# Graph network on one core: one-hots of sources kept in DRAM and read back in later rounds

## The chip, the cores and the metric

The program runs on one core of a Trainium2 chip. Its engines run beside each other and wait on semaphores: PE (matmuls, and transposes by an identity), DVE and ACT (elementwise work), POOL (here it issues the gathers) and SP (here it issues most loads and stores). Sixteen DMA engines move the data. The metric is the device time of one execution in microseconds (us); three runs took 7040.45, 7045.45 and 7043.78, median 7043.78.

## The reference

A graph of 3125 nodes with 64 features and 103,125 edges, sorted by destination, goes through four blocks, each followed by adding its input and a layer norm:

```python
norm = deg_inv[src] * deg_inv[dst]                       # 1 round: sum
out  = segment_sum(norm[:, None] * x[src], dst)
ke   = k[src] + edge_attr @ we                           # 2 rounds: attention
a    = exp(score - segment_max(score, dst)[dst])         # score = (q[dst] * ke).sum / 8
out  = segment_sum(a / denom[dst] * (v[src] + e), dst) + x @ ws + bs
msg  = (h @ weight)[src, rel_type] * edge_weight         # 1 round: relations
h    = relu(cat(x[dst], x[src] - x[dst]) @ W1 + b1) @ W2 + b2
x    = relu(segment_max(h, dst))                         # 3 rounds: maximum
```

Every round needs the row of each edge's source node, x[src], for all edges.

## The kernel before

Edges lie in 808 tiles of 128; four tiles make a chunk of 512 edges, 202 chunks in all. The attention rounds take one chunk a step (202 steps). The sum, relation and maximum rounds pair a chunk of the first half with one of the second and take 101 steps of eight tiles. Between rounds a stage works on the nodes in seven groups of blocks and writes the next round's table of source rows (src_table) and, for attention and maximum, of destination rows (dst_table).

A tile's source rows come in one of two ways. POOL gathers them by an indirect DMA, 128 rows of 256 bytes (`gather`, L1194, and `gather_att`, L1201). Or they are picked on PE: DVE compares the tile's 128 source numbers with all 25 x 128 node numbers and writes a one-hot of 128 x 3200 bytes in fp8 (`make_onehot`, L1752); PE multiplies its 25 blocks with the table, which lies in SBUF split into three bf16 parts (`split_table`, L851 to L854), into one PSUM bank (`pick`, L1456: 25 matmuls of 192 columns a tile); DVE adds the three parts and puts the rows where a gather would have (`place_rows`, L1763). The sum round picks one tile in eight from step 4 on; a maximum round picks one and two tiles in turn from step 1 on. Attention and relations gather everything. There are two buffers for one-hots.

The order on every engine is written out by `chunks`: in step t a stage with lag k works on chunk t - k, and the stages of a step stand in the order of the list. Waits are on semaphores, and an engine or a DMA queue that waits holds up all that stands behind it.

In an attention round SP's step for chunk c (`fetch_att`) loads the one-hots of destinations every fourth chunk (L1103), then four windows of destination rows (L1109), and for even c the edge features of chunks c and c + 1 (L1112). The last of these waits until DVE has weighed chunk c - 7, whose slot is reused:

```python
wait(sp, (q.weighted, c - UA + 2))      # UA = 8 slots
```

PE makes a chunk's queries from the windows (`query`, L1494); DVE multiplies them with keys (`product`, L1813); once a group of four chunks is through the softmax, DVE weighs a chunk's rows (`weigh`, L1877) and PE turns them (L1549); a scan over the edges follows (L1774), PE turns its result back (`back`, L1565), ACT copies it out and stores it. DVE weighs chunk c - 5 in the step in which it forms the product of chunk c.

Of the kernel before, what the change touches and what calls it, by code (L numbers as in the profile page):

```python
# [26 lines left out]
P = 128  # L27
TC = 4
# [3 lines left out]
CH = C // 2  # L32
# [30 lines left out]
PICKS = {"sum": (4, (1,)), "max": (1, (1, 2))}  # L63


def gnn_kernel(nc, src, typ, wgt, dst_row, dst_prev, dst_tile, first, edge_t, x, W, out):
# [21 lines left out]
    src_rows = dram("src_rows", (CH, 2, P), f32)  # L88
    states = [dram("states_sum", (EP, D), f32), dram("states_att", (EP, KA), f32)]

    ctx = ExitStack()
    with ctx:
# [3 lines left out]
        def sem(name):  # L96
# [21 lines left out]
        wrel = sb("wrel", [P, R, D])  # L118
# [51 lines left out]
                  for r, t in {0: flat_agg, 4: tab_a, 5: wide_x, 6: tab_a}.items()}  # L170
# [67 lines left out]
        pick_ps = ps[:, 4, 0:2 * PARTS * D]  # L238
        last_ids = ps[0:1, 6:8, :].rearrange("p b f -> p (b f)")
# [32 lines left out]
        cols_made, cols_turned, rows_made = sem("cols_made"), sem("cols_turned"), sem("rows_made")  # L272
        src_rows_stored = sem("src_rows_stored")
        table_split = sem("table_split")
        ids_copied = sem("ids_copied")
# [56 lines left out]
        class Round:  # L332

            def __init__(self, r, kind):
                self.r, self.kind = r, kind
                self.steps = CH if kind in PAIRED else C
                C_ = self.steps

# [37 lines left out]
                if kind == ATT:  # L376
                    self.rows_ready = [shared(f"rows_ready_a{s_}", 16 * TC * len(range(s_, C, UA))) for s_ in range(UA)]
# [6 lines left out]
                else:  # L384
                    self.first_pick, pattern = PICKS.get(kind, (C_, (0,)))
                    self.picks = [pattern[(c - self.first_pick) % len(pattern)] if c >= self.first_pick else 0
                                  for c in range(C_)]
                    self.most = max(pattern)
                    self.rows_ready = [shared(f"rows_ready_{s_}", self.gathered((C_ - 1 - s_) // U * U + s_))
                                       for s_ in range(U)]  # L390
                if kind in PICKS:
                    picks, self.span = sum(p > 0 for p in self.picks), PB // self.most
                    self.src_loaded = [shared(f"src_loaded_{h}", 16 * len(range(self.first_pick + h * self.span, C_,
                                                                                2 * self.span))) for h in range(2)]
# [16 lines left out]
            def gathered(self, c):  # L411

                return 16 * sum(2 * TC - self.picks[t] for t in range(c % U, c + 1, U))

            def before(self, c):

                return sum(self.picks[0:max(c, 0)])
# [1536 lines left out]
```

## Time and profile before

| | |
|---|---|
| Median of three runs | 7043.78 us |
| Profiled execution | 7051.56 us, span 7049.7 |
| Busy share of the span | POOL 72%, DVE 63%, PE 62%, ACT 23% |
| Gathers (L1194 and L1201) | 5109 |
| One-hots made (L1752) | 547, 1887.8 us of DVE |
| Pick matmuls on three tables (L1456) | 547 x 25 |
| Mean granted clock of PE | 0.767 |

The rounds follow one another with short node stages between: POOL's gathers of the results (L1223) begin at 986 us for the sum round and at 2043 for the first attention round, those of the second end at 3165; the relation round follows, and the three maximum rounds get their first rows at 4336, 5243 and 6150. In the profile's lines an engine's busy time says little by itself, since rounds differ; each round is read apart. "issue" is time in which an engine waited for nothing that the profile shows. SPq is an instruction of SP that issues a DMA; its duration is that of the issue, not of the transfer. A granted clock of 1.00 is 2.4 GHz, 0.50 is 1.2 GHz.

### The profile page before, as it was taken

How to read it: one execution, taken by the hardware profiler on the slowest of the kernel's cores; microseconds unless marked ns; L12 is line 12 of the kernel's file. 1: busy time of each engine (PE TensorE's matmuls, PEld its weight loads, DVE VectorE, ACT ScalarE, POOL GpSimd, SP SyncE). 2: the span in 40 equal slices, each digit the busy share in tenths (PEclk: the TensorE clock that was granted, in tenths of full speed). 3: DMA queues.
4: the chain of work that ended last, by engine and by line, in shares of the span. 5: the costliest groups of instructions: out<-in, count | busy, mean ns of one | idle time of the engine just before them, and what ended most of it. 6: DMA issues, size and time to landing. Idle time of an engine off the chain costs nothing. (4 is left out here: it accounts for less than half of the span.)

```text
span 7049.7 us, 104267 instructions
## 1 busy us (share of the span) xinstructions
PE 4355.2 (62%) x31312; PEld 3479.8 (49%) x31312; DVE 4410.3 (63%) x5581; ACT 1607.1 (23%) x2960; POOL 5057.5 (72%) x5327
## 2 busy tenths in 40 slices
PE   2555546666666556564111125888878888788886
PEld 2554545555565555552111113666656666566664
DVE  7777756666655666662122125777767777677777
ACT  0111113333332333332000001222222222222222
POOL 5777767777757777764777776777767777677776
PEclk9777766666665676666555556999989999899998
DMA  8666656777766777763222224655545655555554
GB/s 168 176 175 176 176 126 134 145 148 149 145 120 134 146 149 145 147 128 104 59 57 59 59 57 91 136 134 134 134 109 136 136 132 135 116 131 133 136 134 108
DMA packets 2145262, 901.73 MB, mean 128 GB/s; under 512 B 1793543, under 2 KB 2004660, under 8 KB 2138308
## 3 DMA queue, kind: packets, MB, share of 16 engines
q1 hardware_dynamic: 1065012, 466.62, 28.7%
q10 hardware_dynamic: 909808, 252.48, 15.8%
q0 software_dynamic: 169888, 175.97, 13.9%
q8 instruction: 259, 4.24, 0.3%
q14 instruction: 295, 2.42, 0.1%
HBM read 625.25 MB, written 269.09 MB: 127 GB/s over the span
## 5 line engine op out<-in xcount | busy, mean ns | idle before, releaser
L1194 POOL DMA_INDIRECT edges_a<-src_table,idx x3493 | 3325.0, 952 | 1287.6 <-issue 1063.4
L1752 DVE TENSOR_TENSOR early<-src_b,ps 128x3200 fp8e4<-128x3200 f32 x547 | 1887.8, 3474 | 576.1 <-PE ps L1456 500.2
L1201 POOL DMA_INDIRECT edges_a<-src_table,idx x1616 | 1530.6, 947 | 536.3 <-issue 458.9
L1470 PE MATMUL ps<-ident,edges_a 128*128 128x128 f32 x808 | 206.8, 405 | 1232.3 <-DVE edges_a L1795 836.7
L1456 PE MATMUL ps<-tab_a,early 128*128 128x192 bf16 x7500 | 699.6, 256 | 253.2 <-DVE edges_a L1763 234.5
L1456 PEld LDWEIGHTS ps<-tab_a,early 128*128 128x128 fp8e4 x7500 | 648.8, 102 | 307.0 <-DVE edges_a L1763 280.0
L1470 PEld LDWEIGHTS ps<-ident,edges_a 128*128 128x128 f32 x808 | 133.0, 202 | 1297.0 <-DVE edges_a L1795 878.2
L1813 DVE TENSOR_TENSOR prod<-ps,edges_a 128x388 f32<-128x388 f32 x404 | 224.9, 557 | 734.8 <-DMA edges_a<-src_table,idx 350.9
L1494 PE MATMUL ps<-win_sb 128*128 128x97 f32 x3232 | 645.4, 364 | 28.3 <-DMA win_sb<-dst_table 28.1
L1565 PE MATMUL ps<-ident,st 128*128 128x128 f32 (+1 forms) x3636 | 649.3, 314 | 5.9 <-DVE st L1774 5.7
L1565 PEld LDWEIGHTS ps<-ident,st 128*128 128x128 f32 (+1 forms) x3636 | 549.6, 176 | 168.0 <-issue 157.1
L1278 ACT ACTIVATE hb<-ps 128x512 f32<-128x512 f32 x505 | 296.2, 587 | 1435.7 <-PE ps L1565 1435.4
L1272 ACT ACTIVATE dst_b<-sel 128x1024 f32<-128x1024 fp8e4 x303 | 320.6, 1058 | 1301.9 <-DMA sel<-onehots 1212.2
L1494 PEld LDWEIGHTS ps<-win_sb 128*128 128x128 f32 x3232 | 597.5, 276 | 38.2 <-DMA win_sb<-dst_table 32.0
L1483 PE MATMUL ps<-dst_b,win_sb 128*64 128x128 f32 x4848 | 535.5, 299 | 0.0
L1795 DVE TENSOR_TENSOR edges_a<-edges_a,wgt_sb 128x256 f32<-128x256 f32 x202 | 77.5, 425 | 712.6 <-DMA edges_a<-src_table,idx 712.6
L1774 DVE TENSOR_TENSOR_SCAN st<-dst_b,st,ps 97x512 f32<-97x512 f32 x402 | 508.2, 1264 | 5.1 <-PE ps L1565 5.1
L1774 DVE TENSOR_TENSOR_SCAN st<-edges_a,st,ps 128x512 f32<-128x512 fp8e4 x200 | 255.7, 1279 | 355.0 <-PE ps L1470 229.7
L1549 PE MATMUL ps<-ident,weighted 128*97 128x128 f32 x1616 | 368.0, 367 | 169.4 <-DVE weighted L1877 167.8
L1456 PE MATMUL ps<-wide_x,early 128*128 128x192 bf16 x3750 | 349.6, 256 | 126.6 <-DVE edges_a L1763 117.5
L1456 PEld LDWEIGHTS ps<-wide_x,early 128*128 128x128 fp8e4 x3750 | 324.3, 102 | 153.4 <-DVE edges_a L1763 140.5
L1480 PE MATMUL ps<-ident,edges_a 128*128 128x128 f32 x1212 | 383.1, 316 | 15.6 <-DMA edges_a<-src_table,idx 15.6
(229 smaller groups left out, 5317.7 us busy)
## 6 DMA issues: line engine op xcount, KB each, us to landing
states_sum<-hb ACTq DMA_DIRECT2D x505, 256.0 KB
edges_a<-src_table,idx POOLq DMA_INDIRECT x5109
win_sb<-dst_table SPq DMA_DIRECT2D x1616, 48.5 KB
states_att<-hb ACTq DMA_DIRECT2D x202, 388.0 KB
dst_b<-in_dst_row SPq DMA_DIRECT2D x50, 1024.0 KB, 12.0
src_b<-src_rows SPq DMA_DIRECT2D x174, 256.0 KB
sel<-onehots SPq DMA_DIRECT2D x305, 128.0 KB
win_sb<-dst_table ACTq DMA_DIRECT2D x1212, 32.0 KB
```

Of the source, the lines that this page charges most:

```text
L1194: pool.indirect_dma_start(rows[:, u, j * D:(j + 1) * D], None, srcs[q.r], bass.IndirectOffsetOnAxis(ap=idx[:, h, at:at + 1], axis=0))\
L1201: pool.indirect_dma_start(xe_a[:, s, j * KA:j * KA + D], None, srcs[q.r], bass.IndirectOffsetOnAxis(ap=idx_a[:, s, j:j + 1], axis=0))\
L1272: nc.scalar.activation(sel_f[:, v, :], sel[:, v, 0:2 * EC], ACT.Copy).then_inc(q.sel_wide.sem, 1)
L1456: last = nc.tensor.matmul(pick_ps[:, at:at + PARTS * D], onehot_b[:, i % 2, b, :], tables[q.r][:, b, :, :].rearrange("p k f -> p (k f)"), ...
L1470: last = nc.tensor.matmul(bank(TURNED, s)[:, j * P:(j + 1) * P], rows[:, v, j * P:(j + 1) * P], ident[:, :], is_transpose=True, start=True ...
L1480: nc.tensor.matmul(bank(TURNED, s)[:, at_j], rows[:, s, j * P:(j + 1) * P], ident[:, :], is_transpose=True, start=True, stop=False)
L1483: last = nc.tensor.matmul(bank(TURNED, s)[h * D:h * D + D, at_j], win_pair(s, j, h), sel_f[:, s, h * EC + j * P:h * EC + (j + 1) * P], sta ...
L1494: last = nc.tensor.matmul(bank(TURNED, s)[:, j * KA:(j + 1) * KA], wide_a[:, s % V, j * P:(j + 1) * P], win_att(v, j), start=True, stop=True)
L1549: last = nc.tensor.matmul(bank(QUERY, s)[0:KA, j * P:(j + 1) * P], weighted[:, s % V, j * KA:(j + 1) * KA], ident[:, :], is_transpose=True ...
L1565: last = nc.tensor.matmul(bank(BACK, s)[:, j * w:(j + 1) * w], st[0:w, s % V, j * P:(j + 1) * P], ident[0:w, 0:w], is_transpose=True, star ...
L1752: nc.vector.tensor_tensor(onehot_b[:, i % 2, :, :], src_b[:, h, o:o + P].unsqueeze(1).to_broadcast([P, NB, P]), ids_ps.unsqueeze(2).to_bro ...
L1774: nc.vector.tensor_tensor_scan(st[0:w, s % V, :], d0, d1, init, op0, op1).then_inc(q.st_ready.sem, 1)
```

## The change

The one-hots of the sum round (97, one for each step from 4 on) are now stored to DRAM, in `hots` (97 of 409,600 bytes), and loaded in the later rounds instead of being made anew.

- Sum round: as before one tile of eight is picked; which half it comes from alternates with the step. SP stores each one-hot (`store_hot`), and DVE waits for the store of two one-hots ago before it overwrites the buffer.
- Attention rounds: chunks with an odd number, from the fifth chunk of each half on, have their last tile picked with the one-hot of the sum round: 97 of 202 chunks, 97 tiles of 808 a round. SP loads the one-hot (`fetch_hot`) behind `fetch_att` of the same chunk. PE picks chunk t at the end of step t, and all its other stages lag two steps more than before; DVE likewise, with `place_rows` at lag 1. The table is split for both rounds (in tab_a and late). The bank for the way back is now one in place of two, the other holds the picked rows.
- Maximum rounds: from step 4 on two, two and one tiles in turn, 162 a round where 150 were. The first of a step is by the loaded one-hot, the second by one that DVE makes (65 a round where 150 were), in a buffer of its own.
- The relation weights share memory with the second attention table and are loaded after that round's last pick; the source numbers for one-hots are laid out for alternating halves.

On SP, in an attention round (L1112 is L1150 now, L1091 is L1129, L1109 is L1147): from the edge load of an even chunk to the end of the next, odd chunk. Before:

```order
L1112 DMA edges_a<-edge_rows 128x8x32 [waits weighted_rows]
L1091 DMA sel<-flags 128x2048 [waits near_out]
L1105 TENSOR_LOAD first_i [waits query_ready]
L1109 ISA
L1109 DMA win_sb<-dst_table 128x97
...
L1105 TENSOR_LOAD first_i [waits query_ready]
```

Now:

```order
L1150 DMA edges_a<-edge_rows 128x8x32 [waits weighted_rows]
L1129 DMA sel<-flags 128x2048 [waits near_out]
L1143 TENSOR_LOAD first_i [waits query_ready]
L1147 ISA
L1147 DMA win_sb<-dst_table 128x97
...
L1086 DMA early<-hots 128x3200 [waits picked]
L1143 TENSOR_LOAD first_i [waits query_ready]
```

The load of the odd chunk's one-hot (early<-hots) is the last of its step, behind the edge load, which waits for weighted rows, and the chunk's four window loads.

On PE, in an attention round: the end of a group's softmax (weight_t), the turning of weighted rows, the way back and the next query (L1494, now L1543). Before:

```order
L1533 MATMUL ps<-kept_row,ones_row 97x16 [waits weighted_rows,kept_out,kept_ready]
L1542 MATMUL ps<-ident,weight_t 128x16 [waits kept_out,weight_ready]
L1549 MATMUL ps<-ident,weighted 97x128 [waits st_ready,weighted_rows]
L1549 MATMUL ps<-ident,weighted 97x128 x3
L1565 MATMUL ps<-ident,st 128x97 [waits hb_ready,st_ready]
L1565 MATMUL ps<-ident,st 128x97 x3
L1494 MATMUL ps<-win_sb 128x97 [waits prod_ready,sel_wide,in_ready_a2]
L1494 MATMUL ps<-win_sb 128x97 x3
```

Now:

```order
L1582 MATMUL ps<-kept_row,ones_row 97x16 [waits weighted_rows,kept_out,kept_ready]
L1591 MATMUL ps<-ident,weight_t 128x16 [waits kept_out,weight_ready]
L1598 MATMUL ps<-ident,weighted 97x128 [waits st_ready,weighted_rows]
L1598 MATMUL ps<-ident,weighted 97x128 x3
L1614 MATMUL ps<-ident,st 128x97 [waits hb_ready,st_ready]
L1614 MATMUL ps<-ident,st 128x97 x3
L1506 MATMUL ps<-tab_a,early 128x192 [waits hot_moved_1,placed]
L1506 MATMUL ps<-tab_a,early 128x192 x24
L1543 MATMUL ps<-win_sb 128x97 [waits prod_ready,sel_wide,in_ready_a2]
L1543 MATMUL ps<-win_sb 128x97 x3
```

The pick of 25 matmuls (L1506), which waits for the loaded one-hot (hot_moved), stands between the way back and the next chunk's query.

On DVE, in a maximum round: one-hots (L1752, now L1810), placing (L1763, now L1829) and scans (L1774, now L1839). Before, two steps:

```order
L1752 TENSOR_TENSOR early<-src_b,ps 128x3200 [waits picked,src_loaded_0]
L1763 TENSOR_REDUCE edges_a<-ps 128x128 [waits turned,picked]
L1774 SCALAR_TENSOR_TENSOR st<-pen,st,ps 128x512 [waits back,st_ready,bars_ready_2,lifted]
L1752 TENSOR_TENSOR early<-src_b,ps 128x3200 [waits picked,src_loaded_0] x2
L1763 TENSOR_REDUCE edges_a<-ps 128x64 [waits turned,picked]
L1774 SCALAR_TENSOR_TENSOR st<-pen,st,ps 128x512 [waits back,st_ready,bars_ready_3,lifted]
```

Now, three steps:

```order
L1810 TENSOR_TENSOR late<-late,ps 128x3200 [waits picked,src_loaded_0]
L1829 TENSOR_REDUCE edges_a<-ps 128x64 [waits turned,picked]
L1839 SCALAR_TENSOR_TENSOR st<-pen,st,ps 128x512 [waits back,st_ready,bars_ready_0,lifted]
L1810 TENSOR_TENSOR late<-late,ps 128x3200 [waits picked,src_loaded_1]
L1829 TENSOR_REDUCE edges_a<-ps 128x128 [waits turned,picked]
L1839 SCALAR_TENSOR_TENSOR st<-pen,st,ps 128x512 [waits back,st_ready,bars_ready_1,lifted]
L1829 TENSOR_REDUCE edges_a<-ps 128x128 [waits turned,picked]
L1839 SCALAR_TENSOR_TENSOR st<-pen,st,ps 128x512 [waits back,st_ready,bars_ready_2,lifted]
```

Three one-hots in two steps became two in three steps, each in the buffer `late`.

The diff, cut to its core:

```diff
-PICKS = {"sum": (4, (1,)), "max": (1, (1, 2))}
+PICKS = {"sum": (1,), "att": (1,), "max": (2, 2, 1)}
+FIRST_PICK = 4
...
+    hots = dram("hots", (CH, P, NB * P), u8)
...
-                  for r, t in {0: flat_agg, 4: tab_a, 5: wide_x, 6: tab_a}.items()}
+                  for r, t in {0: flat_agg, 1: tab_a, 2: late, 4: tab_a, 5: wide_x, 6: tab_a}.items()}
...
-        src_b = sb("src_b", [P, 2, PB * P])
+        src_b = late[:, R * D:R * D + 2 * PB * P].rearrange("p (h e) -> p h e", h=2)
...
+        extra_b = late[:, 0:NB * P // 4].bitcast(f8).rearrange("p (b e) -> p b e", e=P)
...
+        pick_att = ps[:, 7, 0:PARTS * D]
...
+                pattern = PICKS.get(kind, (0,))
+                if kind == ATT:
+                    self.picks = [int(c % 2 == 1 and c % CH >= FIRST_PICK) for c in range(C)]
+                else:
+                    self.picks = [pattern[(c - FIRST_PICK) % len(pattern)] if c >= FIRST_PICK else 0 for c in range(C_)]
...
+            def slots(self, c):
+                if self.kind == ATT:
+                    return [TC - 1] * self.picks[c]
+                return [2 * TC - 1 - c % 2, 2 * TC - 2 + c % 2][0:self.picks[c]]
...
+                wait(sp, (q.picked, q.picks_up_to(q.steps - 1)))
+                for h in range(2):
+                    sp.dma_start(wrel[h * D:(h + 1) * D, :, :], W["rel"].rearrange("r d o -> d r o")).then_inc(wrel_loaded, 16)
...
+                dve.wait_ge(pens_stored, 32)
+                groups((0, scaled), (1, normed), (2, split))
             elif r == 1:
-                groups((0, alpha))
+                groups((0, alpha), (2, split))
...
+                def store_hot(c, s, n):
+                    if not q.picks[c]:
+                        return
+                    i = q.picks_up_to(c) - 1
+                    wait(sp, (q.onehot_made, i + 1))
+                    sp.dma_start(hots[c], onehot_b[:, i % 2, :, :].rearrange("p b e -> p (b e)").bitcast(u8))\
+                        .then_inc(q.hot_stored[i % 2].sem, 16)
+                def fetch_hot(c, s, n):
+                    if not q.picks[c]:
+                        return
+                    i = q.picks_up_to(c) - 1
+                    wait(sp, (q.picked, i - 1))
+                    sp.dma_start(onehot_b[:, i % 2, :, :].rearrange("p b e -> p (b e)").bitcast(u8), hots[c % CH])\
+                        .then_inc(q.hot_loaded[i % 2].sem, 16)
...
-                    chunks(sp, q.steps, (0, fetch_src), (0, fetch_batch), (0, fetch_quad), (2, store_quad), ring=2 * U)
+                    chunks(sp, q.steps, (0, fetch_src), (0, fetch_batch), (0, fetch_quad), (1, store_hot), (2, store_quad), ring=2 * U)
                 elif k == REL:
                     chunks(sp, q.steps, (0, fetch_batch), ring=2 * U)
                 elif k == ATT:
-                    chunks(sp, q.steps, (0, fetch_att), (GC, fetch_near), ring=UA)
+                    chunks(sp, q.steps, (0, fetch_att), (0, fetch_hot), (GC, fetch_near), ring=UA)
                 else:
-                    chunks(sp, q.steps, (0, fetch_src), (0, fetch_pair), (1, fetch_bars))
+                    chunks(sp, q.steps, (0, fetch_src), (0, fetch_pair), (0, fetch_hot), (1, fetch_bars))
...
-                    for j in range(TC):
+                    for j in range(TC - q.picks[c]):
...
-                    if c == q.first_pick:
-                        pe.wait_ge(table_split, q.tables_split)
-                    wait(pe, (q.placed, q.picks_up_to(c - 1)))
-                    for k_, i in enumerate(range(q.before(c), q.before(c + 1))):
-                        wait(pe, (q.onehot_made, i + 1))
-                        at = (1 - k_) * PARTS * D
+                    i = q.picks_up_to(c) - 1
+                    if i == 0:
+                        pe.wait_ge(table_split, 4 * G * q.split_at)
+                    wait(pe, (q.placed, i))
+                    for row, slot in enumerate(q.slots(c)):
+                        if row == MAIN and k != SUM:
+                            wait(pe, (q.hot_loaded[i % 2], 16 * (i // 2 + 1)))
+                        else:
+                            wait(pe, (q.onehot_made, q.most_up_to(c)))
+                        onehot = onehot_b[:, i % 2, :, :] if row == MAIN else extra_b
+                        out_of = pick_of(slot)
                         for b in range(NB):
-                            last = nc.tensor.matmul(pick_ps[:, at:at + PARTS * D], onehot_b[:, i % 2, b, :],
-                                                    tables[q.r][:, b, :, :].rearrange("p k f -> p (k f)"),
+                            last = nc.tensor.matmul(out_of, onehot[:, b, :], tables[q.r][:, b, :, :].rearrange("p k f -> p (k f)"),
...
-                    wait(pe, (q.st_ready, c + 1), (q.hb_ready, c - V + 1))
+                    wait(pe, (q.st_ready, c + 1), (q.hb_ready, c if k == ATT else c - V + 1))
                     w = P if k in PAIRED else kw
                     for j in range(TC):
-                        last = nc.tensor.matmul(bank(BACK, s)[:, j * w:(j + 1) * w],
+                        last = nc.tensor.matmul(bank(BACK, 0 if k == ATT else s)[:, j * w:(j + 1) * w],
...
-                    chunks(pe, q.steps, (0, query), (2, turn_run), (1, turn_scores), (2, group_weights),
-                           (2 + LATE_GROUP, last_weights), (LW + 1, turn_weighted), (LW + 3, back), (1, turn_ends), ring=UA)
+                    chunks(pe, q.steps, (2, query), (4, turn_run), (3, turn_scores), (4, group_weights),
+                           (4 + LATE_GROUP, last_weights), (LW + 3, turn_weighted), (LW + 5, back), (3, turn_ends),
+                           (0, pick), ring=UA)
...
+                    if not q.picks[c] or k == MAX and q.picks[c] == 1:
+                        return
+                    h, use = (c - FIRST_PICK) // PB % 2, (c - FIRST_PICK) // PB // 2
+                    o, i = (c - FIRST_PICK) % PB * P, q.picks_up_to(c) - 1
+                    wait(dve, (q.src_loaded[h], 16 * (use + 1)))
+                    if k == SUM:
+                        wait(dve, (q.picked, i - 1), (q.hot_stored[i % 2], 16 * (i // 2)))
+                    else:
+                        before = max((t for t in range(c) if q.picks[t] > 1), default=-1)
+                        wait(dve, (q.picked, q.picks_up_to(before)))
+                    nc.vector.tensor_tensor(onehot_b[:, i % 2, :, :] if k == SUM else extra_b,
+                                            src_b[:, h, o:o + P].unsqueeze(1).to_broadcast([P, NB, P]),
+                                            ids_ps.unsqueeze(2).to_broadcast([P, NB, P]), ALU.is_equal,
+                                            saturate=False).then_inc(q.onehot_made.sem, 1)
...
+                    if k == ATT:
+                        wait(dve, (q.picked, i), (q.weighted, c - UA + 1))
+                        nc.vector.reduce_sum(xe_a[:, s, (TC - 1) * KA:(TC - 1) * KA + D],
+                                             pick_att.rearrange("p (k f) -> p f k", k=PARTS), axis=AX.X)\
+                            .then_inc(q.placed.sem, 1)
...
-                    wait(dve, (q.query_ready, c + 1), (q.rows_ready[s], 16 * TC * (n + 1)),
+                    wait(dve, (q.query_ready, c + 1), (q.rows_ready[s], q.gathered(c)),
+                         *([(q.placed, q.picks_up_to(c))] if q.picks[c] else []),
...
-                    chunks(dve, q.steps, (2, differences), (0, product), (1, segments), (LW + 2, accumulate),
-                           (LW, weigh), (1, running), ring=UA)
+                    chunks(dve, q.steps, (4, differences), (1, place_rows), (2, product), (3, segments), (LW + 4, accumulate),
+                           (LW + 2, weigh), (3, running), ring=UA)
```

## Rows read from the trace of the kernel before

**Rows 1.** Busy time by stretch: us, each engine (instructions), granted clock, DMA share, GB/s
```profile
200.00:880.00 680.00, 368.18 (x2707) 338.74 (x2705) 504.33 (x857) 73.76 (x174) 515.33 (x541) 0.77 0.69 175
1120.00:1960.00 840.00, 510.52 (x2978) 464.13 (x2979) 544.42 (x1028) 274.71 (x588) 635.36 (x671) 0.68 0.76 146
4400.00:5120.00 720.00, 619.14 (x5363) 452.25 (x5360) 562.98 (x295) 191.00 (x275) 530.74 (x561) 0.97 0.60 135
```

**Rows 2.** The page's costliest groups: the attention rounds' gathers
```profile
L1201 POOL DMA_INDIRECT edges_a<-src_table,idx x1616 | 1530.6, 947 | 536.3 <-issue 458.9
```

**Rows 3.** The chain of waits in a maximum round: start us, us, what
```profile
4583.45 5.97 PE ps L1456 x50
...
4651.71 5.96 PE ps L1456 x50
```

**Rows 4.** Timeline, one group of four chunks in the first attention round: start, duration
```profile
1501.60 0.56 DVE L1813 TENSOR_TENSOR prod<-ps,edges_a 128x388 f32<-128x388 f32 x1 [3.81 <-DMA edges_a<-src_table,idx]
...
1504.61 0.52 DVE L1877 TENSOR_TENSOR weighted<-edges_a,ps 128x388 f32<-128x388 f32 x1
...
1505.16 0.38 SPq L1112 DMA_DIRECT2D edges_a<-edge_rows  x1
...
1506.05 1.88 SPq L1109 DMA_DIRECT2D win_sb<-dst_table  x4
...
1508.46 0.42 SPq L1103 DMA_DIRECT2D sel<-onehots  x1
...
1510.16 1.91 PE L1494 MATMUL ps<-win_sb 128*128 128x97 f32 x8
...
1512.11 0.56 DVE L1813 TENSOR_TENSOR prod<-ps,edges_a 128x388 f32<-128x388 f32 x1 [2.64 <-PE ps L1494]
...
1513.35 0.63 ACT L1267 ACTIVATE win_sb<-sel 128x512 f32<-128x512 fp8e4 x1 [2.45 <-DMA sel<-onehots]
...
1514.37 0.53 DVE L1877 TENSOR_TENSOR weighted<-edges_a,ps 128x388 f32<-128x388 f32 x1
...
1514.93 0.38 SPq L1112 DMA_DIRECT2D edges_a<-edge_rows  x1
...
1515.88 1.06 PE L1494 MATMUL ps<-win_sb 128*128 128x97 f32 x8
...
1516.55 4.67 SPq L1109 DMA_DIRECT2D win_sb<-dst_table  x8
...
1521.19 0.56 DVE L1813 TENSOR_TENSOR prod<-ps,edges_a 128x388 f32<-128x388 f32 x1 [3.09 <-DMA edges_a<-src_table,idx]
```

**Rows 5.** The 256 KB stores of one-hots in the sum round (line 1078)
```profile
DMA to landing us min/median/max: 1.9/3.6/12.5
```

**Rows 6.** The page's DMA issues: KB each, median us from issue to landing
```profile
dst_b<-in_dst_row SPq DMA_DIRECT2D x50, 1024.0 KB, 12.0
```

**Rows 7.** Timeline of PE in the sum round: picks behind an idle stretch
```profile
505.70 3.44 PE L1456 MATMUL ps<-agg,early 128*128 128x192 bf16 x25
...
515.18 3.81 PE L1456 MATMUL ps<-agg,early 128*128 128x192 bf16 x25
```

**Rows 8.** Timeline of a maximum round: one-hot, PE's other work, scan, short pick
```profile
4605.89 0.27 PE L1480 MATMUL ps<-ident,edges_a 128*128 128x128 f32 x1
...
4606.16 3.49 DVE L1752 TENSOR_TENSOR early<-src_b,ps 128x3200 fp8e4<-128x3200 f32 x1 [3.27 <-issue]
...
4610.04 1.27 DVE L1774 TENSOR_TENSOR_SCAN st<-pen,st,ps 128x512 f32<-128x512 bf16 x1
...
4610.18 2.24 PE L1456 MATMUL ps<-tab_a,early 128*128 128x192 bf16 x25 [0.26 <-DVE edges_a L1763]
```

**Rows 9.** Busy time and granted clock within the group of rows 4
```profile
1498.90:1501.40 2.50, 0.00 (x0) 0.00 (x0) 0.00 (x0) 0.32 (x1) 1.89 (x3) 1.00 0.98 199
1508.50:1515.00 6.50, 6.50 (x33) 6.46 (x34) 3.73 (x6) 2.18 (x5) 4.97 (x6) 0.50 0.93 186
```

**Rows 10.** Groups by line: the last operation of a table's split
```profile
L854 DVE TENSOR_TENSOR tab_a<-gy,tab_a 128x256 bf16<-128x256 f32 (+1 forms) x14 | 5.6, 397 | 0.5
```

More of the change, by code:

```diff
@@ L384, in __init__ @@
                 else:
[L385 to L388, printed above, removed]
                     self.rows_ready = [shared(f"rows_ready_{s_}", self.gathered((C_ - 1 - s_) // U * U + s_))
@@ L411, in gathered, with most_up_to @@
             def gathered(self, c):
-                return 16 * sum(2 * TC - self.picks[t] for t in range(c % U, c + 1, U))
-            def before(self, c):
-                return sum(self.picks[0:max(c, 0)])
-            def step_of(self, i):
-                return next((c for c in range(self.first_pick, self.steps) if self.before(c + 1) > i), 0) if i >= 0 else -1
-            def picks_up_to(self, c):
-                return max(c - self.first_pick + 1, 0)
+                ring, n = (UA, TC) if self.kind == ATT else (U, 2 * TC)
+                return 16 * sum(n - self.picks[t] for t in range(c % ring, c + 1, ring))
+            def picks_up_to(self, c):
+                return sum(p > 0 for p in self.picks[0:max(c + 1, 0)])
+            def most_up_to(self, c):
+                return sum((p > 1 if self.kind == MAX else p > 0) for p in self.picks[0:max(c + 1, 0)])
+            def slots(self, c):
+                if self.kind == ATT:
+                    return [TC - 1] * self.picks[c]
+                return [2 * TC - 1 - c % 2, 2 * TC - 2 + c % 2][0:self.picks[c]]
         rounds = [Round(r, k) for r, k in enumerate(ROUNDS)]
@@ L1141, in _ @@
                         sp.wait_ge(bars_stored, 32)
-                    if k == MAX:
-                        fetch_src(q.first_pick - q.span, 0, 0)
+                    if r == 1:
+                        for h in range(2):
+                            wait(sp, (rounds[0].hot_stored[h], 16 * len(range(h, rounds[0].picks_up_to(CH - 1), 2))))
                     wait(sp, *tables_stored(q))
                 if k == SUM:
-                    chunks(sp, q.steps, (0, fetch_src), (0, fetch_batch), (0, fetch_quad), (2, store_quad), ring=2 * U)
+                    chunks(sp, q.steps, (0, fetch_src), (0, fetch_batch), (0, fetch_quad), (1, store_hot), (2, store_quad), ring=2 * U)
                 elif k == REL:
@@ L1191, in gather @@
                     wait(pool, *sources_stored(q), (q.idx_ready, 2 * n + h + 1), (q.turned, c - U + 1))
-                    for j in range(2 * TC - q.picks[c]):
+                    for j in range(2 * TC):
+                        if j in q.slots(c):
+                            continue
                         at = u * 2 * TC + j
@@ L1676, in _ @@
             assert made[0] == PRE_SCALED
[L1678 to L1680 removed]
+            for row in (MAIN, EXTRA):
+                for odd in range(2):
+                    first_tile, n = (odd + (CH if row == odd else 0)) * TC + TC - 1, len(range(odd, CH, 2))
+                    nc.vector.tensor_copy(cols_f[:, row, odd:CH:2], src_i[:, first_tile:first_tile + (n - 1) * 2 * TC + 1:2 * TC])\
+                        .then_inc(laid_out, 1)
             done = [0]
```

106 lines of the change are left out of this document (54 added, 52 removed).

## The prediction

> **What bounds the kernel now.** All durations are from the profiled execution, 7051.6 us with a span of 7049.7; it lies 7.8 us above the median of the three runs (7043.8), so the sum starts at 7051.6 and 7.8 comes off at the end. I read the busy time round by round first. The reader should divide each stretch by POOL's count: 680 us for 541 gathers in the sum round is 1.257 us each, 840 for 671 in the first attention round is 1.252, 720 for 561 in a maximum round is 1.283 [rows 1]. One gather keeps POOL busy for 0.947 us and the idle before it is nearly all "issue" (458.9 of 536.3 us over 1616 gathers, 0.28 each), so 1.25 is POOL's own pace [rows 2]. In the sum and attention rounds POOL therefore sets the time. The maximum rounds are different. The chain of waits runs there through DVE's one-hots and PE's picks, and from one pick of 50 matmuls with a hitch (5.97 us) to the next, eight steps later (every second step picks 50), it takes 68.26 us, 8.53 a step [rows 3]; POOL needs 6.5 gathers or 8.14 a step, so it sits just behind.
>
> Then one group of four chunks in the attention round, engine by engine [rows 4]. DVE's product at 1501.60 and that at 1521.19 are one group apart (on the mean 16 gathers, 20.03 us). DVE idles 3.09 us for gathered rows and 2.64 for PE's query: this is all the slack it has. Now SP: the chunk's weighing ends at 1504.61 + 0.52 = 1505.13 and the edge load starts at 1505.16; the other ends at 1514.90 and the next edge load starts at 1514.93. SP stands at the edge load until DVE lets it go, and everything behind it in SP's program waits too.
>
> **The change part by part.** *Gathers.* Attention loses 97 of 808 gathers a round (odd chunks from the fifth of each half), maximum rounds 162 - 150 = 12, the sum round none. If POOL stayed the bound, attention would give back 97 x 1.252 = 121 us a round.
>
> *A new cycle in attention.* On SP the load of a chunk's one-hot stands behind the window loads of the same odd chunk c+1, and those behind the edge load of chunk c, which waits for DVE to weigh chunk c-7. DVE weighs c-7 after its product of c-2; that needs PE's query of c-2; and the query stands on PE behind the pick of c-1, which waits for the previous one-hot. So every pick hangs on the load before it, once per two chunks, and nothing in this ring can run ahead, though there are two buffers. Two turns make a group:
>
> SP, weighing to the issue of the load: 1505.13 to the end of four window loads at 1506.05 + 1.88 = 2.80 us; in the other half a load of flags lies between, and half of the eight window loads (4.67/2) ends at 1518.89, 3.99 after 1514.90. Together 6.8 [rows 4].
> Landing, twice. No row shows a 400 KB load into 128 rows of 3200 bytes. The nearest is the 256 KB load of one-hots on the same queue, issued at 1508.46; ACT, which idled 2.45 us for it, starts at 1513.35: 4.9 us [rows 4]. In the sum round stores of 256 KB land in 1.9 to 12.5 us, median 3.6 [rows 5], and loads of 1024 KB in 12.0 [rows 6]. My ends are 1.9 and 12.0. I take 4.5, next to 4.9 because the rings are emptier when the round is slower: 9.0.
> Pick, twice: 25 matmuls took 3.44 and 3.81 us where PE had idled before them [rows 7] and 2.24 at full clock [rows 8]. PE will idle for the load before each pick. In the group of [rows 4] PE had no matmul from 1498.9 to 1501.4; the granted clock was then 0.50 (the level of 1.2 GHz) through 6.5 us of unbroken work up to 1515.0 [rows 9]. I take 3.6: 7.2.
> Query, twice: 1.06 at full clock, 1.91 at half [rows 4]; taken 1.5: 3.0.
> Product to the end of weighing: 3.53 (1501.60 to 1505.13) and 2.79 (1512.11 to 1514.90): 6.3 [rows 4].
> Sum 32.3 us a group against 20.03, so 12.3 more. With 97 picks a round, 48.5 groups: 597 us a round, 1193 for two. The 121 us of gathers are not subtracted, since POOL then waits. By the low ends (1.9, 2.24, 1.06) a group takes 23.5 us and two rounds 340 more, by the high ends (12.0, 3.81, 1.91) 48.5 and 2760 more. Only with landing, pick and query together at 3.5 us per pair of chunks, where I have 9.6, would the ring be as fast as now.
>
> The Trainium skill ("DMA: Bandwidth & Descriptors", Anatomy of one DMA) puts a transfer of the gpsimd path at about 2.0 us plus its bytes over 436 GB/s; by this page 409,600 bytes would land in 2.9 us, an estimate. The trace disagrees for less data: 4.9 us for 256 KB on SP's queue [rows 4]. By the page's figure the group would be 29.1 us and the kernel 7825.
>
> *Maximum rounds.* DVE makes 65 one-hots a round in place of 150, 3.49 us each [rows 8], two per three steps. DVE's work per three steps falls to 2 x 3.49 + 3 scans of 1.27 and three small reductions, some 12 us, and it leaves the chain. Late next are two engines that nearly tie. POOL: 19 gathers per three steps, 23.8 us, 7.93 a step. PE: from 4605.89 to 4609.92 its other work takes 4.03 a step, and five thirds of a pick at 2.24 make 3.73; a pick of 50 that takes 5.96, 1.5 more than twice 2.24, comes once in eight steps [rows 3] and adds 0.2: 7.95. I take 8.1, since they also wait for each other: 0.43 x 97 = 42 us less, and steps 1 to 3, which lose their picks, cost 8 x 1.252 - 8.53 = 1.5 more each: 37 a round, 112 for three. Ends: 50 a round less, or no gain. The one-hot loads have room here: SP may issue one when the pick two steps back is done, a whole step and the next step's other work, some 10 us, before it is needed.
>
> *Edits that cost little.* The 97 stores in the sum round: a buffer comes back two steps later, 17.6 us, against 3.6 plus the 12.0 of a load ahead in the queue; POOL's pace hides them, taken 0, and some 60 us if the cover fails now and then. Two more tables to split: seven groups of four operations of at most 0.40 us, 11 us a table [rows 10], half of it beside the waits between rounds: 12 for both. The bank for the way back has no second buffer now: PE returns to it a chunk later, cost 0; uncovered it would be one ACT copy like the 0.63 [rows 4] for 404 chunks, 255 us. The later load of the relation weights lies beside the emptying of the pipeline, the four layout copies for two are small: 0.
>
> Sum: 7051.6 + 1193 - 112 + 12 - 7.8 = 8137, said as 8135.
>
> **The rivals.** *The loads come in time and POOL stays the bound.* Place: the same ring in attention; it decides if a one-hot lies in the buffer before PE comes to the pick. Then 2 x 121 us go, and 112: 6700, faster. For it: DVE's idle 3.09 us a group is more than the 2.5 us that two gathers give back, and the product was moved two chunks later to make room. Against: the order on SP, which that shift does not touch: the load still leaves after the weighing, and PE's pick follows about one transposition after the same weighing. Chance 0.06.
> *The loads come in time but PE is the bound.* PE gets 7.2 us of picks a group, of which half stands ahead of a query for which DVE already waits 2.64; 20.03 - 3.09 + 3.6 = 20.5 a group, 46 more in two rounds, 112 less in maximum rounds: 6990. For it: PE has no idle stretch there except its waits. Against: as above. Chance 0.04.
> *The loads queue like the 1024 KB loads,* behind 1024 rows of 128 bytes of the edge load: 12.0 us, a group of 47.3, 2645 more: 9590. Against: these loads are 2.5 times as large. Chance 0.06.
>
> **How the numbers follow.** The ring has 0.84. Its own range: low, landing 3.0, pick 2.24 and query 1.06, a group of 25.7 and 550 us, with the best maximum rounds 7450; high, landing 6.5 and the high ends, a group of 37.5 and 1700, with half the gain and 60 in the sum round 8750. That is also the range I give: outside it lie the three rivals, 0.16, and a little of the ring's ends. Faster by over 0.2% (what a measurement of this kernel can tell from no change) are the two rivals in which the loads come in time, 0.10; within 0.2% only a ring far below my low end, 0.01; slower the rest, 0.89.
>
> **What would show it.** Right: both attention rounds stretch to some 1600 us with POOL at about 2.3 us a gather; PE's first matmul of an attention pick waits for the one-hot's load, several us each; on SP the load is issued some 3 to 4 us after a weighing; the granted clock stays low there. Maximum rounds near 8.1 us a step with DVE about half busy, and the sum round at 1.26 us a gather. Wrong: attention picks that never wait for a load, or attention rounds of 900 us. A landing other than 4.5 moves the time by 194 us for each us.

## The result, and the profile after

The changed kernel takes 8214.51 us (median of 4 runs, 8205.36 to 8227.14) against 7043.97 for the kernel before (four runs): 1.166 times as long [1.164, 1.168]. The forecast was slower, 8135. The profiled execution has a span of 8219.7 us, 1170.0 more than before.

The first gather of a round's last rows marks where each round ends. From mark to mark (POOL's rows in both traces; the last line is from the last mark to the end of the span):

| stretch, us | before | after | difference | forecast |
|---|---|---|---|---|
| sum round, from the start | 985.6 | 1023.5 | +37.9 | 0 |
| attention 1 | 1057.5 | 1688.7 | +631.2 | +597 |
| attention 2 | 1082.1 | 1725.9 | +643.8 | +597 |
| relation round | 1151.2 | 1164.5 | +13.3 | 0 (12 for the splits, anywhere) |
| maximum 1 to 3 | 894.9, 908.8, 907.8 | 860.0, 854.4, 855.9 | -34.9, -54.4, -51.9 | -37 each |
| tail | 61.7 | 46.7 | -15.0 | 0 |

So the time went where it was forecast, into attention. Busy time by stretch, after; the columns are those of [rows 1], and the three rows answer to the three there (sum, attention, maximum):

```profile
200.00:880.00 680.00, 329.57 (x2550) 297.97 (x2551) 474.79 (x799) 66.53 (x162) 499.69 (x525) 0.74 0.78 211
1200.00:2600.00 1400.00, 758.46 (x5047) 686.09 (x5048) 575.50 (x1115) 287.98 (x594) 562.77 (x595) 0.70 0.51 112
...
5740.00:6340.00 600.00, 570.01 (x5131) 425.99 (x5129) 299.61 (x201) 171.12 (x247) 453.55 (x480) 0.99 0.76 186
```

Again divide by POOL's count. Attention: 1400 / 595 = 2.35 us a gather, where POOL's own pace is 1.25. The DMA share fell from 0.76 to 0.51, so the DMA engines do not set the pace there. Maximum round: 600 / 480 = 1.250, POOL's pace; with 19 gathers in three steps that is 7.92 a step, and DVE is half busy. The sum round went from 1.257 to 1.295.

The page's costliest groups, after; the first row answers to [rows 2]:

```profile
L1242 POOL DMA_INDIRECT edges_a<-src_table,idx x1422 | 1345.2, 946 | 1984.6 <-DVE weighted L1943 1555.8
L1506 PE MATMUL ps<-tab_a,early 128*128 128x192 bf16 x7275 | 829.1, 284 | 502.5 <-DMA early<-hots 493.0
...
L1822 DVE TENSOR_REDUCE edges_a<-ps 128x64 f32<-128x192 f32 x194 | 69.4, 358 | 1692.0 <-PE ps L1506 1692.0
```

POOL's idle time was 536.3 us, nearly all "issue"; now it is 1984.6 and ends on DVE's weighing. DVE in turn idles 1692.0 us for PE's picks, and PE before the picks for the one-hots' load. Read in that order, the three rows are the ring. Here is one group of four chunks on the timeline, two turns of it, from product to product (columns as in [rows 4]):

```profile
1502.05 0.56 DVE L1879 TENSOR_TENSOR prod<-ps,edges_a 128x388 f32<-128x388 f32 x1 [1.35 <-PE ps L1543]
...
1505.06 0.52 DVE L1943 TENSOR_TENSOR weighted<-edges_a,ps 128x388 f32<-128x388 f32 x1
...
1505.61 0.38 SPq L1150 DMA_DIRECT2D edges_a<-edge_rows  x1
...
1506.52 2.08 SPq L1147 DMA_DIRECT2D win_sb<-dst_table  x4
...
1508.65 0.44 SPq L1086 DMA_DIRECT2D early<-hots  x1
...
1514.49 4.16 PE L1506 MATMUL ps<-tab_a,early 128*128 128x192 bf16 x25 [3.73 <-DMA early<-hots]
...
1518.44 1.33 PE L1543 MATMUL ps<-win_sb 128*128 128x97 f32 x8
...
1519.81 0.56 DVE L1879 TENSOR_TENSOR prod<-ps,edges_a 128x388 f32<-128x388 f32 x1 [0.76 <-PE ps L1543]
...
1522.07 0.53 DVE L1943 TENSOR_TENSOR weighted<-edges_a,ps 128x388 f32<-128x388 f32 x1
...
1522.63 0.38 SPq L1150 DMA_DIRECT2D edges_a<-edge_rows  x1
...
1526.12 0.42 SPq L1086 DMA_DIRECT2D early<-hots  x1
...
1530.23 4.16 PE L1506 MATMUL ps<-tab_a,early 128*128 128x192 bf16 x25 [6.56 <-DMA early<-hots]
...
1534.18 1.91 PE L1543 MATMUL ps<-win_sb 128*128 128x97 f32 x8
...
1536.13 0.56 DVE L1879 TENSOR_TENSOR prod<-ps,edges_a 128x388 f32<-128x388 f32 x1 [1.35 <-PE ps L1543]
```

The group takes 34.08 us. Each link starts where the one before ends: weighing done at 1505.58, edge load at 1505.61; landed and picked, then the query, then the product 0.04 us after it.

Cut at five events, a turn is edge load to one-hot load (SP), to the pick (landing), the pick, its end to the product (query), and the product to the next edge load. Means over 190 turns of both attention rounds, here and for three runs that change one term (left out are the first turn of each round and the one from round to round):

| us | SP | landing | pick | query | product to edge load | turn | turns |
|---|---|---|---|---|---|---|---|
| forecast | 3.40 | 4.50 | 3.60 | 1.50 | 3.15 | 16.15 | |
| after | 3.33 | 4.87 | 4.07 | 1.35 | 3.18 | 16.80 | 190 |
| e5: load ahead of windows | 0.75 | 5.31 | 3.85 | 1.08 | 3.18 | 14.17 | 190 |
| e4: half the pick | 3.33 | 4.97 | 2.24 | 1.64 | 3.18 | 15.36 | 190 |
| e10: half the load | 3.32 | 4.07 | 3.95 | 1.08 | 3.18 | 15.61 | 190 |

### The profile page after: what moved, and what is told of

It reads as the page before. It is cut to its first block and busy times, and to the rows that moved or that the text cites. A ratio compares the mean times of both kernels' runs of the same rounds, so it can differ in the third digit from the quotient of the medians.

```text
span 8219.7 us, 116161 instructions
## 1 busy us (share of the span) xinstructions
PE 4951.0 (60%) x37062; PEld 4020.5 (49%) x37062; DVE 3656.5 (44%) x5569; ACT 1628.0 (20%) x2960; POOL 4837.6 (59%) x5097
## 3 DMA queue, kind: packets, MB, share of 16 engines
q1 hardware_dynamic: 1165668, 684.79, 32.3%
## 5 line engine op out<-in xcount | busy, mean ns | idle before, releaser
L1235 POOL DMA_INDIRECT edges_a<-src_table,idx x3457 | 3289.3, 951 | 1238.5 <-issue 1031.8
L1242 POOL DMA_INDIRECT edges_a<-src_table,idx x1422 | 1345.2, 946 | 1984.6 <-DVE weighted L1943 1555.8
L1506 PE MATMUL ps<-tab_a,early 128*128 128x192 bf16 x7275 | 829.1, 284 | 502.5 <-DMA early<-hots 493.0
L1506 PEld LDWEIGHTS ps<-tab_a,early 128*128 128x128 fp8e4 x7275 | 744.4, 113 | 559.3 <-issue 514.8
L1810 DVE TENSOR_TENSOR late<-late,ps 128x3200 fp8e4<-128x3200 f32 x195 | 677.6, 3475 | 331.9 <-PE ps L1506 321.9
L1822 DVE TENSOR_REDUCE edges_a<-ps 128x64 f32<-128x192 f32 x194 | 69.4, 358 | 1692.0 <-PE ps L1506 1692.0
L1506 PE MATMUL ps<-late,early 128*128 128x192 bf16 x2425 | 396.2, 359 | 496.5 <-DMA early<-hots 496.5
L1839 DVE TENSOR_TENSOR_SCAN st<-pen,st,ps 128x512 f32<-128x512 bf16 x300 | 383.4, 1278 | 537.3 <-PE ps L1606 536.2
L1506 PEld LDWEIGHTS ps<-late,early 128*128 128x128 fp8e4 x2425 | 341.7, 144 | 540.4 <-issue 516.8
L1506 PE MATMUL ps<-agg,early 128*128 128x192 bf16 x2425 | 317.9, 311 | 383.5 <-DVE edges_a L1829 383.5
L1543 PE MATMUL ps<-win_sb 128*128 128x97 f32 x3232 | 533.9, 318 | 21.1 <-DMA win_sb<-dst_table 21.1
L1543 PEld LDWEIGHTS ps<-win_sb 128*128 128x128 f32 x3232 | 499.9, 236 | 29.5 <-DMA win_sb<-dst_table 23.1
L1839 DVE TENSOR_TENSOR_SCAN st<-dst_b,st,ps 97x512 f32<-97x512 f32 x402 | 508.3, 1264 | 5.2 <-PE ps L1614 4.6
L1506 PEld LDWEIGHTS ps<-agg,early 128*128 128x128 fp8e4 x2425 | 281.4, 125 | 413.6 <-DVE edges_a L1829 401.3
```

Source lines behind the costliest of these rows:

```text
L1235: pool.indirect_dma_start(rows[:, u, j * D:(j + 1) * D], None, srcs[q.r], bass.IndirectOffsetOnAxis(ap=idx[:, h, at:at + 1], axis=0))\
L1242: pool.indirect_dma_start(xe_a[:, s, j * KA:j * KA + D], None, srcs[q.r], bass.IndirectOffsetOnAxis(ap=idx_a[:, s, j:j + 1], axis=0))\
L1506: last = nc.tensor.matmul(out_of, onehot[:, b, :], tables[q.r][:, b, :, :].rearrange("p k f -> p (k f)"), start=b == 0, stop=b == NB - 1)
L1543: last = nc.tensor.matmul(bank(TURNED, s)[:, j * KA:(j + 1) * KA], wide_a[:, s % V, j * P:(j + 1) * P], win_att(v, j), start=True, stop=True)
L1810: nc.vector.tensor_tensor(onehot_b[:, i % 2, :, :] if k == SUM else extra_b, src_b[:, h, o:o + P].unsqueeze(1).to_broadcast([P, NB, P]), i ...
L1839: nc.vector.tensor_tensor_scan(st[0:w, s % V, :], d0, d1, init, op0, op1).then_inc(q.st_ready.sem, 1)
```

## The experiments

The kernel before, run again beside e1 to e4, beside e5 to e8 and beside e9 and e10, took 7056.47, 7046.96 and 7046.79 us in the median, so a difference between runs of different sets may be off by some 10 us. Ratios are taken against the kernel before of the same set.

**e5, e4, e10: one term of the ring each.** All three start from the changed kernel.

```diff
-  chunks(sp, q.steps, (0, fetch_att), (0, fetch_hot), ...)   # e5
+  chunks(sp, q.steps, (0, fetch_hot), (0, fetch_att), ...)
```

> The changed kernel with one edit: in the attention rounds the load of an odd chunk's one-hot goes ahead of the four window loads of the same chunk, and stays behind the edge load of the chunk before. Theory: the ring stays closed, and only its term on SP falls, from 3.07 + 3.52 = 6.6 us a group (weighing to the issue of the load) to about 1.2: 97 groups in two rounds x 5.4 less = 524, so 7690 (7600 to 7800, since the landing may change with what lies ahead of it in the queue). Rival (what the earlier load of run e1 cured was not the ring but one long landing behind the window loads): the ring's gain is as large as e1's, below 7100. Rival (SP's part is not in the ring): 8150 to 8230.

Measured: 7708.31 us, 506 less. The load now leaves SP at once:

```profile
1509.77 0.38 SPq L1150 DMA_DIRECT2D edges_a<-edge_rows  x1
...
1510.82 0.43 SPq L1086 DMA_DIRECT2D early<-hots  x1
...
1516.12 3.66 PE L1506 MATMUL ps<-tab_a,early 128*128 128x192 bf16 x25 [5.31 <-DMA early<-hots]
```

From edge load to one-hot load 1.05 us (3.04 and 3.49 in the rows of after above), and PE waits for the load as before. The ring is shorter and still closed.

```diff
-  for b in range(NB):
+  nb = 13 if k == ATT else NB                            # e4
+  for b in range(nb):
```

> One edit: in the attention rounds a pick multiplies 13 of the 25 blocks (the other blocks' rows are left out of the result); the loads keep their bytes and their place on SP. Theory (the ring, with two picks per four chunks in it): a pick falls from 4.16 us to about 2.2, and 97 picks a round x 2 rounds x 2.0 = 390 us go: 7825, between 7750 and 7900. Rival (the loads' traffic sets the pace): no change, 8150 to 8230.

Measured: 7946.88, 268 less, outside the range expected (7750 to 7900). That is short of the 390 because the pick fell by 1.83 us and not 2.0, the query behind it grew by 0.29 and the landing by 0.10.

```diff
-  sp.dma_start(onehot_b[:, i % 2, :, :] ..., hots[c % CH])
+  nb = 13 if k == ATT else NB                            # e10
+  sp.dma_start(onehot_b[:, i % 2, 0:nb, :] ..., hots[c % CH][:, 0:nb * P])
```

> The changed kernel with one edit: in the attention rounds the load of a one-hot brings 13 of the 25 blocks (208 of 400 KB; the other blocks keep what lay in the buffer); its place on SP, the pick and the rest stay. The ring turns 194 times, so the time moves by 194 us for each us of landing. If the landing grows with the bytes as the 1024 KB load's 12.0 us against the 400 KB load's 5.0 has it (0.011 us a KB), 2.2 us and 420 us go: 7795. If the landing is mostly the wait behind the small packets that lie ahead, it falls by under 0.5 us: 8110 to 8215. In either case the fall in the time over 194 is the fall in the landing that the trace shows. Rival (the bytes themselves, not the landing in the ring, cost the time): the attention rounds lose half of their extra, 630 us: 7580.

Measured: 7998.44, 216 less, between the first two cases. The landing fell by 0.80 us for 192 KB. The turn fell by 1.19: against what was expected, the landing alone does not account for the fall in the time, since the query also took 0.27 and the pick 0.12 less.

Taken together: in e5, e4 and e10 the turn shortened by 2.63, 1.44 and 1.19 us, which over 194 turns is 511, 280 and 231 us. From mark to mark the two attention rounds lost 503, 277 and 227, the kernel 506, 268 and 216. e5 changes neither the bytes nor PE's work, e4 only the work, e10 only the bytes, and all three have one price: each us in a turn costs about 180 to 190 us of the kernel.

**e1, e2: the ring opened.**

```diff
-  chunks(sp, q.steps, (0, fetch_att), (0, fetch_hot), ...)
+  chunks(sp, q.steps, (-1, fetch_hot), (0, fetch_att), ...)   # e2: -2
```

> One edit: in the attention rounds SP issues the load of an odd chunk's one-hot at the start of the step before it, ahead of that step's window and edge loads; the bytes, the picks and the buffers stay. Theory (the ring closes on SP's order): the load now hangs on the weighing two chunks earlier, so it and the pick before it come once per four chunks instead of twice. From the profile of the changed kernel a turn is then query 1.6 + product to weighing 3.2 + SP 3.3 + landing 5.0 + pick 4.2 = 17.2 us per four chunks, about POOL's 14 gathers x 1.25 = 17.5, and a group takes 18 to 20 us instead of 34.1: 97 groups x 14 to 16 less, 6640 to 6860, if PE at its low clock is the bound up to 7000. Rival (the loads' bytes or PE's extra work cost the time, wherever the load stands): 7900 to 8250.

> As the run before, but the load is issued one step earlier still, ahead of the window loads of the chunk two before it. Theory of SP's order: the last link of the ring from a pick to the next load is the buffer alone; if the run before is bound by POOL or PE the time is the same as there within 0.5%, if it is still bound by the ring it falls further, to 6640 to 6800. Rival (bytes or PE's work): as slow as the changed kernel, 7900 to 8250.

Measured: 6975.75 and 6991.47, 0.989 [0.987, 0.991] and 0.991 [0.989, 0.993] of the kernel before: inside the 7000 that was given for PE as the bound, not in the 6640 to 6860, and within 0.5% of each other. With the same bytes and picks in another order the 1171 us are gone; that the kernel is a little faster than before comes from the maximum rounds, as e3 shows. Who waited for the load's line, in us and times, in the changed kernel and then in e1:

```profile
  PE ps L1506: 989.6, 192
```
```profile
  PE ps L1506: 0.5, 1
```

But a group takes 20.47 us, where POOL's 14 gathers need 17.5. One group of e1, the picks, POOL's waits and the load:

```profile
1501.88 0.94 POOL L1242 DMA_INDIRECT edges_a<-src_table,idx  x1 [2.85 <-DVE weighted L1943]
...
1502.01 2.23 PE L1506 MATMUL ps<-tab_a,early 128*128 128x192 bf16 x25
...
1504.61 0.42 SPq L1086 DMA_DIRECT2D early<-hots  x1
...
1511.75 0.44 SPq L1086 DMA_DIRECT2D early<-hots  x1
...
1513.80 4.05 PE L1506 MATMUL ps<-tab_a,early 128*128 128x192 bf16 x25
...
1522.35 0.94 POOL L1242 DMA_INDIRECT edges_a<-src_table,idx  x1 [3.27 <-DVE weighted L1943]
```

The pick that starts at 1513.80 uses the load of 1504.61; the one of 1511.75 is for the pick after it. POOL waits once a group for a weighing that stands behind a query behind a pick. e2 issues earlier still and gains nothing; there PE waits 177.4 us for windows that now stand behind the load, against 48.8 in e1.

**e3: no attention picks.**

```diff
-  self.picks = [int(c % 2 == 1 and c % CH >= FIRST_PICK) for c in range(C)]
+  self.picks = [0] * C
```

> One edit: attention chunks pick nothing and gather all four tiles, as before the change; the sum round still stores its one-hots and the maximum rounds load them. Theory: the attention rounds go back to 1057 and 1082 us from 1689 and 1727, so the time is 8214 - 1276 = 6938, and what is left against the 7044 of before, some 106 us less, is the maximum rounds' 35 + 54 + 52 less the sum round's 38. Rival (part of the loss sits outside the attention picks, in the third split or the single bank of the way back): 7050 or more.

Measured: 6946.01 (expected 6938). From mark to mark the attention rounds take 1062.0 and 1083.7, so the third split and the single bank of the way back cost 6 us in both rounds together. The maximum rounds stay at 859.6, 854.3 and 857.0. It is 30 us faster than e1: two picks a group, even with their loads in time, are worse than none.

**e6, e7, e8: what bounds e1.** e6 is e1 with 13 blocks a pick; e7 and e8 are e1 with one pick per four chunks:

```diff
-  int(c % 2 == 1 and c % CH >= FIRST_PICK)
+  int(c % 4 == 1 and c % CH >= FIRST_PICK)      # e7; e8: c % 4 == 3
```

> The kernel of run e1 (load one step earlier) with a pick of 13 of the 25 blocks in the attention rounds (the other blocks' rows are left out of the result). In e1 a group of four chunks takes 20.4 us while POOL's 14 gathers need 17.5. Theory (PE sets the pace there: its two picks of 4.05 and 2.23 us in a group stand ahead of the queries, and POOL waits for the weighing): 3 us a group go, to POOL's own pace of 17.5 to 17.8, 97 x 2.6 to 2.9 less than 6976: 6690 to 6730. Rival (the loads' bytes or SP's order still set the pace in e1): 6950 to 6990.

Measured: 6844.21 (expected 6690 to 6730). PE's picks do set e1's pace (132 us go; the attention rounds alone lose 134 from mark to mark), but only half of the expected fall comes. Busy time in the first attention round (columns of [rows 1]):

```profile
1200.00:2000.00 800.00, 570.90 (x4040) 526.52 (x4040) 568.05 (x1111) 286.06 (x588) 557.51 (x590) 0.77 0.88 193
```

POOL still takes 800 / 590 = 1.36 us a gather, and still idles for the weighing. What holds the weighing then is open; in these 800 us PE waits 84.5 us for DVE's maxima and 35.1 for windows, and neither was changed by itself.

> The kernel of run e1 with a pick in one chunk of four instead of two (chunks 1, 5, 9, ... of the numbering by fours), so 15 gathers a group and one pick. Theory (PE sets the pace of e1 by 2.9 us a group over POOL): one pick less gives back 2.2 to 4.1 us on PE, POOL needs 15 x 1.25 = 18.8, so a group takes 18.8 to 19.0 instead of 20.4: 6976 - 97 x 1.5 = 6830, 6815 to 6870, and below the run without attention picks (6946). Rival (any attention pick costs PE more than its gather gives POOL): between 6946 and 6976.

> As the run before, but the chunks that pick are 3, 7, 11, ...: the pick that stands elsewhere in the group's softmax. In e1 one of the two picks of a group runs in 2.23 us and the other in 4.05 behind PE's waits of the softmax. Theory: as above, 6815 to 6870, and the two runs differ by at most (4.05 - 2.23) x 97 / 2 = 88 us, in the order of which keeps the short pick; if POOL is the bound in both they agree within 0.3%.

Measured: 6853.21 and 6949.64. e7 came as expected, e8 did not: it is no faster than e3 without picks, and the two differ by 96 us where 88 was the most expected. One pick of e7, and one of e8:

```profile
1502.14 2.23 PE L1506 MATMUL ps<-tab_a,early 128*128 128x192 bf16 x25
```
```profile
1517.88 4.14 PE L1506 MATMUL ps<-tab_a,early 128*128 128x192 bf16 x25
```

Busy time and granted clock (columns as in [rows 9]) of e7 over its pick, and of e8 ahead of its pick and over it:

```profile
1502.10:1504.20 2.10, 2.10 (x28) 2.10 (x27) 1.47 (x3) 1.10 (x3) 1.52 (x2) 1.00 1.14 151
```
```profile
1511.20:1516.00 4.80, 2.62 (x13) 2.14 (x13) 4.53 (x12) 2.57 (x8) 3.77 (x4) 0.54 0.84 220
1517.90:1521.80 3.90, 3.90 (x27) 3.59 (x25) 0.00 (x0) 1.01 (x2) 2.99 (x4) 0.50 0.76 160
```

In e8 the pick stands behind PE's small steps of the group's softmax, where PE was busy 2.62 of 4.80 us and the clock had fallen to about half, the 1.2 GHz level; the pick then runs at 0.50 and takes 1.9 us more. In e7 it runs at the full level. Over all picks the means are 2.27 us at 0.99 (98 picks) and 3.82 at 0.58 (96): some 150 us of PE time, of which 96 show in the kernel's. That the clock makes the whole difference is not shown, since the two places also differ in what waits behind the pick.

**e9: a third buffer for the stores of the sum round,** on top of e7.

```diff
+  hot_of = [onehot_b[:, 0, :, :], onehot_b[:, 1, :, :], extra_b]
-  ... onehot_b[:, i % 2, :, :] ...; hot_stored[i % 2]; (q.picked, i - 1)
+  ... hot_of[i % 3] ...;            hot_stored[i % 3]; (q.picked, i - 2)     # sum round only
```

> The kernel of run e7 (load one step earlier, one attention pick in four chunks) and in the sum round a third buffer for the one-hots that are stored (the extra one-hot's space, unused there). Theory: the sum round of the changed kernel is 38 us longer than before because DVE waits for a store to land before it can write the next one-hot into the same buffer (200 us of waits in 680); with a buffer more that wait goes and so do 30 to 38 us: 6853 - 34 = 6819, 6810 to 6830. Rival (the stores' traffic slows POOL's gathers themselves): 6845 to 6860.

Measured: 6808.21 (expected 6810 to 6830), 45 less than e7, and 0.966 [0.965, 0.967] of the kernel before: the best version here. The sum round is back at 984.1 us (985.6 before), with all 97 stores still made. DVE's waits for a store, in us, times and longest, between 200 and 880 us in the changed kernel and then in e9:

```profile
DVE early L1810 <- DMA hots<-early: 200.1, 33, 10.3
```
```profile
DVE early L1811 <- DMA hots<-early: 0.4, 1, 0.4
```

The edit also lets DVE run one pick further ahead of PE; for PE's picks DVE waited only 11.5 us in that stretch of the changed kernel.

## Why the prediction was right

*The ring.* Right in mechanism, place and nearly in size: 32.3 us a group forecast, 33.6 as the mean of the turns. By terms, SP, the query and the weighing were within 0.15 us a turn. Two were too small. The landing: 4.87 for 4.50. The pick: 4.07 for 3.60; that was taken between two picks of the sum round whose granted clock was 0.64 and 0.57, and here nearly all were at the low level (0.52 as the mean over 193 picks). The clock ahead of and in the pick at 1514.49:

```profile
1504.20:1514.40 10.20, 3.61 (x21) 2.93 (x20) 5.52 (x13) 2.68 (x8) 5.67 (x6) 0.72 0.77 166
1514.49:1518.60 4.11, 4.11 (x26) 3.89 (x27) 0.00 (x0) 0.00 (x0) 0.93 (x1) 0.50 0.17 38
```

PE was busy 3.61 of 10.20 us while it waited, and the pick was granted 0.50 throughout. So this ring makes PE wait ahead of its longest step, and that step then runs at the low clock. Both terms together: (0.37 + 0.47) x 194 = 163 us. Attention came out 1275 - 1193 = 82 above the forecast: the query and SP were shorter by 0.15 and 0.07, 43 us in all, and the other 40 or so lie outside the full turns and were not followed.

*The total.* Its nearness, 8135 for 8214.51, owes something to luck: the sum round's 38 us too much and the maximum rounds' 44 us too little nearly cancel, and what is left of the 80 is attention's 82.

*The landing's source.* I took it from the 256 KB load's 4.9 us [rows 4] rather than by bytes. e10 bears that out: 192 KB less saved 0.80 us, so by the same slope, an estimate from two sizes, all 400 KB account for 1.7 of the 4.87 and 3.2 do not go with the size. The Trainium skill ("DMA: Bandwidth & Descriptors", Anatomy of one DMA) has, for the gpsimd path, a fixed 2.0 us and a bandwidth by which, as estimates, those 192 KB are 0.45 us and the load 2.9. That most of the landing does not go with the bytes agrees with the trace; the landing measured on SP's queue is 1.9 longer, and the measurement decides.

*Maximum rounds.* Right that they leave the chain of one-hots and fall to POOL's pace, too low in gain. I added 0.17 us a step because POOL and PE "also wait for each other"; they did not, and the step is 7.92. With the tail the three rounds gave 156 us for the 112 forecast. From a round's first gather to its last, POOL took 844 to 846 us before and 807.9 after, 36 to 38 less, which is the forecast; the rest came behind the last gather, where DVE's last scan ended 24 to 26 us after the mark before and 9 to 10 after. That part falls into the stretch behind the mark, which is why the first of the three shows only 35 and the tail 15.

*Sum round.* This step failed: "a buffer comes back two steps later, 17.6 us, against 3.6 plus the 12.0 of a load ahead in the queue; POOL's pace hides them, taken 0". The round became 37.9 us longer, inside the 60 that I had set for a cover that fails now and then. The line's instructions on SP's queue, after, min, median and max in ns:

```profile
L1078 SPq DMA_DIRECT2D hots<-early x97: 320/3201/9602, 121.4 to 1012.3; - x97
```

And the landing of these stores in e9, where no one waits for them:

```profile
DMA to landing us min/median/max: 5.8/11.1/17.3
```

I had priced the store by the 3.6 of smaller ones [rows 5] and left out the time for which its issue alone holds SP. In e9 a store is also issued only 4.6 us in the median after DVE has ended the one-hot; with 11.1 to land that is 15.7, where the 17.6 less the 3.5 of making the next one-hot leave 14.1. e9 shows that it was the buffer and not the traffic.

*Splits.* 12 forecast; e3 has 6 in the attention rounds. The relation round's 13 lie between its mark and its first gather (140.2 us, 125.6 before). They are absent in e1, e2, e3, e6, e8 and e9 (1151.0 to 1153.7 from mark to mark) and there in e4, e5, e7 and e10 (1158.6 to 1162.9), so they belong to no edit that was told apart here.

*The rivals.* That the loads would come in time was rightly held unlikely. Had they come, which of the two would have been right is answered by e1: PE as the bound, 6990 forecast, 6975.75 measured; not POOL's 6700. There a group takes 20.47 us for the 20.5 forecast and the two attention rounds 36 more than before for the 46; that the sum is within 15 us is also luck, by the sum and maximum rounds as above. That loads queue like the 1024 KB ones is refuted by the landing. The DMA engines, at 0.51 in attention, did not set its pace.

## What to carry to other kernels

A prefetch runs ahead only as far as the wait that stands before it in its queue's program: with two buffers, the load here still came one turn of its own consumer late, and moving one line by one step was worth 1239 us. Before a gather is traded for a load, follow the load's issue back to the wait ahead of it, and ask whether that wait depends on what the load feeds; if it does, price the turn, not the transfer. Then look at what the work moved to another engine stands behind: where in the group a pick was put (e7, e8) decided whether it paid.

## What was not expected of the hardware

The issue of one 400 KB store holds SP's queue for a median of 3.2 us and up to 9.6, where the loads of the same 400 KB are issued in a median of 0.4 (min, median and max in ns, after):

```profile
L1086 SPq DMA_DIRECT2D early<-hots x485: 331/422/2097, 1093.7 to 8157.0; - x162
```

In e9 the stores' issues take a median of 2.2 and up to 8.9, though no one waits for the store there. In the kernel before, such holds lay on the 1024 KB load of the sum round (up to 8.3 us, median 0.8), which takes at most 1.3 in e9. So the hold is not tied to one transfer; what makes an issue hold was not tested.
